# GNN layer, one core: tile 14 of every third block fetched row by row by SyncE and ScalarE

## The reference, cut to what matters

```python
h = jnp.maximum(_layernorm(x, axis=-1), 0.0)
Qv, Ku = h @ W_Q.T, h @ W_K.T
score = einsum('md,md->m', Qv[dst], Ku[src]) / sqrt(d) * exp(-edge_dt)
w = softmax over the 16 best edges of each dst
agg = segment_sum(w[:, None] * (h[src_s] @ W_msg.T), dst_s, num_segments=n)
return x + relu(h @ W_self.T + agg)
```

## Time and profile before

| | |
|---|---|
| Median of 3 runs (lowest, highest) | 2013.95 us (2012.52, 2016.31) |
| The profiled execution: its time, its span | 2014.03 us, 2011.8 us |
| PE, DVE, ACT, POOL busy | 1403.0, 1487.9, 1074.5, 1491.9 us |
| Indirect DMAs of L615 | 1564 (662 + 437 + 403 + 31 + 31) |
| DMA engines' busy share, 400 to 1900 us | 0.33 |

### The profile page before, as it was taken

One profiled execution on the slowest core, in us unless ns is written; L12 is line 12 of the kernel. 1 busy time (PEld: TensorE's weight loads), 2 busy tenths in 40 slices (PEclk: granted clock), 3 DMA queues, 4 the chain that ended last, 5 costly groups with the idle time before them and its releaser, 6 DMA issues. The chain is left out here.

```text
span 2011.8 us, 45575 instructions
## 1 busy us (share of the span) xinstructions
PE 1403.0 (70%) x15219; PEld 1289.3 (64%) x15220; DVE 1487.9 (74%) x5024; ACT 1074.5 (53%) x3376; POOL 1491.9 (74%) x1577
## 2 busy tenths in 40 slices
PE   1157888777767777676777767677767767677776
PEld 0157888766666666666667666666766766666665
DVE  6668999777677767767676777767777776767766
ACT  2767676554545545454554545455454545555453
POOL 7777777777777777777777777777777777777773
PEclk9968989888888898888888888888888888898888
DMA  8933333333333333333323333333333333333321
GB/s 232 281 95 88 115 106 116 102 89 99 102 86 102 88 100 94 95 102 84 103 86 102 89 99 100 88 102 88 100 96 92 97 91 101 86 102 89 97 74 33
DMA packets 120604, 205.86 MB, mean 102 GB/s; under 512 B 32268, under 2 KB 75922, under 8 KB 120172
## 3 DMA queue, kind: packets, MB, share of 16 engines
q0 software_dynamic: 50112, 102.80, 20.1%
q1 hardware_dynamic: 69627, 97.27, 14.9%
q10 hardware_dynamic: 626, 2.84, 0.4%
HBM read 186.34 MB, written 16.44 MB: 101 GB/s over the span
## 5 line engine op out<-in xcount | busy, mean ns | idle before, releaser
L615 POOL DMA_INDIRECT X<-H_table,idx x662 | 627.3, 948 | 202.7 <-issue 198.7
L1138 ACT ACTIVATE X<-OT,w 128x125 f32<-128x125 bf16 x1792 | 530.0, 386 | 30.8 <-DVE w L955 30.8
L615 POOL DMA_INDIRECT E<-H_table,idx x437 | 414.4, 948 | 136.4 <-issue 130.6
L1106 ACT ACTIVATE OT<-pT 128x512 bf16<-128x512 f32 (+1 forms) x500 | 274.7, 549 | 423.8 <-PE pT L1242 414.2
L615 POOL DMA_INDIRECT Z<-H_table,idx x403 | 382.0, 948 | 123.0 <-issue 119.9
L1242 PE MATMUL pT<-identb,O 125*128 125x128 bf16 x1800 | 211.2, 243 | 270.2 <-DVE X L876 251.0
L1242 PEld LDWEIGHTS pT<-identb,O 125*128 125x128 bf16 x1800 | 135.7, 108 | 319.7 <-issue 269.7
L1231 PE MATMUL pG<-G,O 125*128 125x128 bf16 x3600 | 314.6, 250 | 0.0
L1231 PEld LDWEIGHTS pG<-G,O 125*128 125x128 bf16 x3600 | 276.1, 115 | 0.1
L881 DVE TENSOR_REDUCE s<-X 128x8 f32<-128x1024 f32 x200 | 268.6, 1343 | 0.0
L1267 PE MATMUL pU<-X 128*128 128x125 f32 x1512 | 191.7, 282 | 1.6
(11 more groups left out here) (197 smaller groups left out, 2523.1 us busy)
## 6 DMA issues: line engine op xcount, KB each, us to landing
rawi<-D_table SPq DMA_DIRECT2D x50, 576.0 KB
ewt<-D_table SPq DMA_DIRECT2D x50, 576.0 KB
X<-H_table,idx POOLq DMA_INDIRECT x662
E<-H_table,idx POOLq DMA_INDIRECT x437
Z<-H_table,idx POOLq DMA_INDIRECT x403
hb<-H_table SPq DMA_DIRECT2D x100, 62.5 KB
xb<-in_x SPq DMA_DIRECT2D x100, 62.5 KB
out<-ob SPq DMA_DIRECT2D x100, 62.5 KB
```

The source lines that it names most:

```text
L615: return eng.indirect_dma_start(out=Et[q][:, t * 128:(t + 1) * 128], out_offset=None, in_=x if b < RAW else H, in_offset=bass.IndirectOffs ...
L1106: AT.mark(eng.activation(OT[b % 3][:, q0[g]:q0[g] + GQ[g], :].rearrange("p t n -> p (t n)"), pT[:, 0:GQ[g] * 128], ACT.Copy), b, f"T{g}")
L1138: last = eng.activation(weighted(c)[:, t * 128:t * 128 + NB], OT[c % 3][:, t, 0:NB], ACT.Copy, scale=w[:, t:t + 1])
```

## The change

From block 20 on, every third block (20, 23, ..., 98: 27 blocks) is "owned": GpSimd leaves out its tile 14. Its 128 rows are fetched by 128 ordinary DMAs of one row of 512 bytes each. The row numbers are read into registers from a small SBUF row `own`, which SyncE loads from a new DRAM table `SRC_table`. SyncE issues 30 of the DMAs in each of three rounds, ScalarE 13, 13 and 12. Whoever waited for the gather of tile 14 now waits for a count of 128 landed rows.

```diff
+    OWN = 14
+    EVERY = 3
+    FROM = 20
+    BYSP = 30
+    BYACT = -(-(128 - EVERY * BYSP) // EVERY)
+    HEAD = 5
...
+        def owned(b):
+            return FROM <= b < B and (b - FROM) % EVERY == 0
...
         def landed(eng, b, t):
             if b >= 0:
                 k = t % AHEAD
-                eng.wait_ge(s_gp[k], 16 * ((1 if k < 2 else 2) * b + t // AHEAD + (0 if k == 1 else 1)))
+                if t == OWN and owned(b):
+                    n = owned_before(b)
+                    eng.wait_ge(s_row[n % 2], 16 * 128 * (n // 2 + 1))
+                else:
+                    less = owned_before(b) if k == OWN % AHEAD else 0
+                    eng.wait_ge(s_gp[k], 16 * ((1 if k < 2 else 2) * b + t // AHEAD + (0 if k == 1 else 1) - less))
+
+        def share_of(b):
+            for k in range(EVERY):
+                if owned(b + 1 + EVERY - k):
+                    return b + 1 + EVERY - k, k
+            return None, 0
+
+        def row_numbers(engine, b, lo, hi):
+            return nc.values_load_multi_w_load_instructions(own[owned_before(b) % 2][0:1, lo:hi], engines=[engine], min_val=0, max_val=N - 1,
+                                                            skip_runtime_bounds_check_because="source nodes of the input")[1]
+
+        def fetch_rows(eng, b, lo, rows):
+            for p, row in enumerate(rows):
+                eng.dma_start(Et[b % NE][lo + p:lo + p + 1, OWN * 128:(OWN + 1) * 128],
+                              H[bass.ds(row, 1), :]).then_inc(s_row[owned_before(b) % 2], 16)
...
+            for p, q in RUNS:
+                eng.dma_start(SRC[0, 0:M].rearrange("(p r) -> p r", r=RUN)[p:q, :], src2[p:q, :]).then_inc(s_sc, 16)
+            VS.wait(eng, "msz")
+            eng.dma_start(SRC[0, M:MP].rearrange("(t e) -> t e", e=128), ms[:, :]).then_inc(s_sc, 16)
             meta(LEAD + 1)
             load_h(2)
             spread(2)
+
+            def own_numbers(b):
+                n = owned_before(b)
+                if n == 0:
+                    eng.wait_ge(s_sc, 48)
+                if n >= 2:
+                    AU.wait(eng, b - 2 * EVERY - 3, "U")
+                r = first_edge(mybir.EngineType.SP, b)
+                eng.dma_start(own[n % 2][:, :], SRC[0:1, bass.ds(r + OWN * 128, 128)]).then_inc(s_own, 16)
+
+            def own_rows(b, k):
+                if k == 0:
+                    PM.wait(eng, b - NE, "agg3")
+                    AC.wait(eng, b - NE, "cp")
+                    eng.wait_ge(s_own, 16 * (owned_before(b) + 1))
+                lo, hi = BYSP * k, min(BYSP * (k + 1), 128)
+                fetch_rows(eng, b, lo, row_numbers(mybir.EngineType.SP, b, lo, hi))
...
                 if j + 3 < B:
                     spread(j + 3)
+                if owned(j + 2 + EVERY):
+                    own_numbers(j + 2 + EVERY)
+                b, k = share_of(j)
+                if b is not None:
+                    own_rows(b, k)
                 load_x(j)
...
                 for t in range(1 if b else 0, SURE):
+                    if t == OWN and owned(b):
+                        continue
...
             for b in range(B + 2):
                 c = b - 1
+                own_b, k = share_of(b)
+                if own_b is not None:
+                    lo = BYSP * EVERY + BYACT * k
+                    hi = min(lo + BYACT, 128)
+                    if k == 0:
+                        eng.wait_ge(s_own, 16 * (owned_before(own_b) + 1))
+                    rows = row_numbers(mybir.EngineType.Activation, own_b, lo, hi)
+                    early = HEAD if k else 0
+                    fetch_rows(eng, own_b, lo, rows[0:early])
                 if 0 <= b - 2 < B:
                     mixed(b - 2)
                 if b + 2 < B:
                     turn(b + 2)
+                if own_b is not None:
+                    if k == 0:
+                        PM.wait(eng, own_b - NE, "agg3")
+                    fetch_rows(eng, own_b, lo + early, rows[early:])
```

More of the change, by code:

```diff
@@ L66, in gnn_kernel @@
     CP = [1, 1, 1, 1, 1, 5]
+    OWN = 14
[4 more added lines that the diff above has]
+    HEAD = 5
     H = nc.dram_tensor("H_table", [N, D], f32, kind="Internal").ap()
     D16 = nc.dram_tensor("D16_table", [1, MP], i16, kind="Internal").ap()
+    SRC = nc.dram_tensor("SRC_table", [1, MP], i32, kind="Internal").ap()
     META = nc.dram_tensor("META_table", [4, MP], f32, kind="Internal").ap()
@@ L132, in gnn_kernel @@
         cprow = sb("cprow", [1, 128], i32)
+        own = [sb(f"own{q}", [1, 128], i32) for q in range(2)]
         MR = [sb(f"MR{q}", [128, 128]) for q in range(NM)]
@@ L245, in gnn_kernel @@
         s_relay = sem("s_relay")
+        s_sc = sem("s_sc")
+        s_own = sem("s_own")
+        s_row = [sem(f"s_row{q}") for q in range(2)]
         s_fl = sem("s_fl")
@@ L276, in gnn_kernel, with owned_before @@
         p0 = [sum(GP[:g]) for g in range(4)]
+        def owned(b):
+            return FROM <= b < B and (b - FROM) % EVERY == 0
+        def owned_before(b):
+            return len([c for c in range(b) if owned(c)])
         def landed(eng, b, t):
@@ L298, in gnn_kernel @@
         shares = ["rstd", "nmr", "n", "h"]
-        vn = ["zero", "ident", "identb", "mr0", "msf", "pad16", "pad", "rawd", "neq", "c1", "winr", "win", "wini", "val", "scan",
+        vn = ["zero", "ident", "identb", "mr0", "msf", "pad16", "pad", "msz", "rawd", "neq", "c1", "winr", "win", "wini", "val", "scan",
               "ctmp", "carry", "slot", "cnt2", "rb", "rbrow", "rbf", "al", "alf", "step", "cp"]
@@ L703, in _ @@
             VS.mark(eng.tensor_scalar(pad[:, :], pidx[0:4, 0:1].to_broadcast([4, CAP]), -1.0, None, ALU.mult), "pad")
+            VS.wait(eng, "msf")
+            VS.mark(eng.memset(ms[:, :], 0), "msz")
             eng.wait_ge(s_dst, 48)
```

## The result

| | median us | runs | against before |
|---|---|---|---|
| before | 2014.1 | 2012.52 to 2016.31 | |
| changed | 2064.6 | 2062.66 to 2066.05 | 1.0248 (1.0236 to 1.0261) |

The account below looks back on a forecast made before the run. The prediction took GpSimd's unbroken gathers as the bound, with SyncE's 18.4 us round hidden below 19.15. It summed 2014.0 - 33.7 + 1 = 1981.3, forecasting 1981 us, range 1977 to 2018 us.

Parts of the forecast that it names:

- GpSimd bounds, and 27 gathers are worth 33.7 us: GpSimd has no free time; 27 gathers at 1.25 us each go, 33.7 us off the whole time.
- The register load of 30 values, 0.7 us: On SyncE, one load of 30 row numbers from `own` per round, taken near a single load: 0.7 us.
- each value is a round trip: SyncE's load of `own` pays for each of 29 further values, at most 0.277 us: slower, up to 2547 us; chance 0.17.
- The skill's rule: About 200 ns per register even in bulk: 29 further values 5.8 us, SyncE's round 24.2 us, time about 2370 us.
- A fetch at 0.45 us: On SyncE, each one-row DMA takes 0.45 us from start to start, so 30 take 13.6 us a round.
- The rest of the round (3.7 + 0.4): SyncE's old work, 3.7 us a round, plus loading `own` once in three rounds, 0.4 us a round.
- The formula for a SyncE that is over: For a SyncE round of S beyond 19.4 us, the time is 1980 + 81 x (S - 19.15) - 20.
- The slack of 20 us: SyncE may fall about one round, 20 us, behind once before others feel it, through `spread` and the fetched rows.
- ScalarE is covered: ScalarE's fetches delay it at most 3.9 us, below VectorE's 4.5 us of waiting: no charge; upper bound 22 us.
- The start, 1 us: Three added DMAs ahead of the loop's first loads delay its start by 0 to 2 us, taken as 1.
- the DMA traffic, nothing: The rows are the same bytes the gather moved, with DMA engines at 0.33; no gain or loss charged.
- the three signs named for being wrong: `own` load takes several us; a fetch exceeds 0.5 us; VectorE begins waiting for TensorE while GpSimd stands at `in_step`.

Follow-up runs that it names:

- the aligned cut: The changed kernel with a block's 128 rows cut at multiples of four (SyncE 32, 28, 28; ScalarE 12, 12, 16): 1980.8 us, 0.9828.

## Why the prediction was wrong

- **GpSimd bounds, and 27 gathers are worth 33.7 us:** right. Without any fetching 34.9 us came out.
- **The register load of 30 values, 0.7 us: this step failed.** The prediction took "one instruction that reads 120 adjacent bytes" to be near a single load. The loads took (2.24 + 6.28 + 2.31) / 3 = 3.61 us, 2.9 more. It put the price of each further value between nothing and 0.277 us, took nothing, and said that 0.05 us would decide. The price is 0.055 us for a load that starts on a multiple of four values and 0.20 us elsewhere; the mean of the three loads is (3.61 - 0.7) / 29 = 0.10 us, over the point that the prediction named. Its rival "each value is a round trip" was therefore right in kind, a price for each value, for one load in three, and had the right sign, but was far too dear as priced (2547 us). That the start of a load matters, the prediction had nowhere.
- **The skill's rule:** the Trainium skill, page "Runtime: NRT & Kernel Launch", section "Instruction fetch mechanics", has about 200 ns for each register even in bulk. The page speaks of loads from HBM and these are from SBUF. The 0.20 us of the loads off the multiple of four agree with it; those on it, at 0.055 us, don't, and there the measurement decides. The floor of about 600 ns that the prediction sets beside it is not a floor here: single values took 0.277 and 0.290 us in the earlier trace rows.
- **A fetch at 0.45 us:** a little high, 0.42 was measured, 1.1 us a round less. The rest of the round (3.7 + 0.4) came to 20.43 - 3.61 - 12.5 = 4.3. With the load as measured, the prediction's own sum gives 18.4 + 2.9 - 1.1 + 0.2 = 20.4 us. The 1981 us of the forecast did come out with the aligned cut (1980.8 us), but not for the reason given. The loads there take (2.04 + 1.85 + 1.90) / 3 = 1.93 us and not 0.7, and SyncE's round is back at 4.3 + 1.93 + 12.2 = 18.4 us because 29.3 fetches a round cost 12.2 us. At 0.45 us each they would cost 13.2 and the round 19.4 us, the very edge.
- **The formula for a SyncE that is over:** right to 1.5 us at two lengths of the round. 1980 + 81 x (20.43 - 19.15) - 20 = 2064 us, measured 2064.6; for 19.71 it gives 2005 (2006.4); for 21.82 it gives 2176, 12 us above the 2164.6. The slack of 20 us was argued from the spread and the fetched rows. What the others waited for was the `own` row (213.2 us of ScalarE) and `hb` (67.2 us of TensorE), which the prediction did not list. That these allow about as much lateness is luck.
- **ScalarE is covered:** right at 13, 8 and 8 fetches, since aligning SyncE's load alone brought 1983.7 us, but the account was wrong. It took off the gap of 2 us, then 0.8 us of TensorE's idle time (a figure for which it shows no row), then VectorE's 4.5 us of waiting, 7.3 us together. The run with 24, 20 and 20 rows leaves 5 us a round and no more. The three are therefore best read as one idle time, the wait for gathers, seen on three engines.
- **The start, 1 us, and the DMA traffic, nothing:** no cost showed.
- **What the profile should show:** 1537 gathers at the old pace came as written, and the 30 fetches took 12.5 us, a little under the 13 to 14; the load "below 1.5 us", the wait for fin ahead of `xb` and `Os` "at most 0.3 us later" did not. Two of the three signs named for being wrong came: the load of `own` took several us, and VectorE waited for TensorE (112.4 us on L1016) while GpSimd stood still at `in_step` (81.2 us).

## What to carry to other kernels

When work is moved into the free time of an issuing queue, add up that queue's whole round as if it were an engine's. Here SyncE took the bound over with 20.4 us against 19.15, although the page of the profile never counts it as busy. An operation that the trace shows only at size one is not priced by that row; a probe in a queue's idle time cost nothing here (2013.9 us) and gave the price at every size. And idle time that one bound causes on several engines may be spent once only.

## What the runs showed of the hardware

- A register load on SyncE of n int32 values from SBUF: 0.49 us for one, 0.50 for four, then 0.22 us for each further four and about 0.2 for each value left over, if the first value lies on a multiple of four; 0.20 us for each value otherwise (30 values: 2.27 against 6.28 us). Starts at 5, 6 and 7 were alike (6.28, 6.27, 6.27). Reading 32 values is cheaper than 30 (2.07 us), and beginning two values early and dropping them took the load from 6.28 to 2.08 us.
- ScalarE pays about the same, with more spread between runs: 13 values off the multiple 2.8 to 3.3 us, 12 on it 0.78 to 1.23 us (medians).
- A DMA of one row of 512 bytes with its address from a register goes out every 0.42 us on SyncE and every 0.39 us on ScalarE, while ScalarE's activations that stand before it in the program still run (in the run with 24, 20 and 20 rows a fetch is issued at 1331.50 and a scaled copy starts at 1331.52).
